# A two-layer gated network on one core: waits, weight loads and transform order at the start and at the batch turns

## The chip, the cores and the metric

One core of one Trainium2 chip runs the whole program. The metric is device time in microseconds, the median over executions; lower is better. A profiled execution has a time of its own.

## The reference, cut to what matters

The input `x` has 4 batches of 512 tokens with 512 features, `ctx` is 4 x 512 x 512. Four sublayers follow each other, each on the layer-normed `x` and each added back with a tanh gate:

```python
x = x + tanh(g_xattn[0]) * moe_by_token_id(layernorm(x), tokens, ctx, ctx, ctx)   # 4 experts: silu(x g^T) * (x u^T), then y d^T
x = x + tanh(g_ffn[0])   * hadamard_ffn(layernorm(x))      # fwht, gate and up 2048 wide, silu, fwht, down
x = x + tanh(g_xattn[1]) * wkv(w, u, layernorm(x), ctx)    # recurrence over the 512 tokens
x = x + tanh(g_ffn[1])   * moe_top2(layernorm(x))          # 8 experts, 448 wide, two per token, and a shared one
```

In `hadamard_ffn` the input is multiplied by signs and passed through a Walsh-Hadamard transform, and so is the hidden layer, before `W_down` (512 x 2048).

## The kernel before, in words

Everything is written out by hand: each engine (TensorE, VectorE, ScalarE, GpSimd, SyncE) has its own list of instructions, and semaphores tie the lists together. An engine does its list in order, so a wait holds everything behind it. Products of float32 are made of three products of rounded high parts and low parts (`wh` and `wl`, `xh` and `xl`).

**First sublayer, called attention here (0 to 160 us).** The tokens are sorted by expert into 19 tiles of 128. VectorE makes a one-hot table from the token ids (`ge`, `mask`, L1479 to L1482), TensorE counts ranks with it (L1084 to L1092), VectorE turns them into row numbers (`from_i`, L1531), and GpSimd gathers the rows of `x` with them (`gather`, L545). The four context matrices come in by DMA; ScalarE rounds each of their 16 blocks (`wh`, L827), VectorE makes the rest (`w_low`, L1523). Block `j` belongs to expert `j // 4`. A tile is then normalized (`x_stats`, `x_norm`, L1555 to L1562), turned on TensorE (`x_turn`, L1102), split (`x_high` on ScalarE, `x_low` on VectorE, L1567), and multiplied (L1116). In the kernel before, TensorE waits for all 16 `wl` blocks and for `s_slot` ahead of the first `x_turn`, and the wait for `mask` (`s_gate`, 2) also counts ScalarE's tanh of the gates (L824), which needs two small loads:

```python
pe.wait_ge(s_gate, 2)
pe.wait_ge(s_wl, E0 * DC)
```

**Between the sublayers (160 to 194 us).** TensorE transforms `W_down` in 16 pieces (`w16`, L1146), whose results ScalarE copies (L925). The pieces are loaded by SyncE in 8 transfers of 512 KB (L434, L467), made of rows of 128 floats, that is of 512 bytes, into four places, so that 4 of them wait for places to come free. Meanwhile the results of the first sublayer are gathered back into token order (L564, four tiles for a batch), added (`residual`, L1605), their deviation is inverted by GpSimd (L534), and `x` is normalized (`xnf`, L1675). TensorE turns it (`turn`, L1157; bank `c` gets chunk `c` of all four tiles), ScalarE scales it (L865), VectorE makes two butterfly steps (`half_mix`, `full_mix`, L1626 to L1633), TensorE the last seven of the transform (`mix`, L1162). Before the mixes stand `w16` 12 to 15, the wait for ScalarE's last copy and two transforms of down weights (`prep_w`, L1151).

**Second sublayer and wkv (194 to 762 us).** Four batches of 16 steps: `gate` and `up` (both `product`, L1178), then `down` of the step before (L1206). Steps of batch 0 also prepare the weights (`gu_high`, `gu_low`, `down_scale`) and keep them in DRAM; the steps of batches 1 to 3 run the wkv of the batch before beside them. The last two steps of a batch also make the four mixes of the next one: in batches 1 and 2 mixes 0 and 1 ahead of `up` of step 14, mixes 2 and 3 ahead of `up` of step 15.

**Last sublayer (762 us to the end)** is the mixture of eight experts. The change does not touch it.

SyncE's list around the change: four loads of `x` (L431), after the first four gathers have landed; after all 16 `wl`, four `W_down` loads (L434); the gate and up weights of chunk 0 (`load_wn`, L439); the 19 stores of results (L446); `load_wn(1, .)`; the other four `W_down` loads; then the keeping of chunk 0 (L458).

## Time and profile before

| what | value |
|---|---|
| median of three executions | 1280.11 us (1280.07 to 1285.75) |
| profiled execution: its own time | 1281.66 us |
| profiled execution: span from first to last instruction | 1279.7 us |
| TensorE matmul busy | 1209.8 us, 95% of the span |
| TensorE weight loads, VectorE, ScalarE, GpSimd busy | 1012.2, 666.1, 450.1, 458.2 us |
| chain of waits, share by engine | TensorE 80%, VectorE 8%, DMA 3%, ScalarE 3%, issue 3%, GpSimd 2% |

The span is cut in 40 slices of 32 us; the busy tenths of TensorE and its granted clock read:

```profile
PE   1999979999999999999999998999889999999998
PEclk9999999999999999999999999998999999999999
```

The first digit is the first 32 us, the sixth holds 160 to 192 us. Matmuls are pipelined and their ends are modelled, so starts of successive groups say more than the length of one.

### The profile page before, as it was taken

The page shows a single profiled execution, that of the slowest core. Times are in us where ns is not written, and L with a number is a line of the kernel's source. Part 1 is how long each engine was busy: PE and PEld are TensorE (multiplying, and loading weights), DVE is VectorE, ACT ScalarE, POOL GpSimd, SP SyncE. Part 2 cuts the span into 40 slices and gives each one's busy share as a digit, 9 for nine tenths or more (in the row PEclk, how much of TensorE's full clock was granted, in tenths as well). Part 3 has the DMA queues.
Part 4 walks back from the last instruction along what each step waited for, and adds up shares of the span by engine and source line. Part 5 has one row for each costly group of instructions (what it writes and reads, how often), then busy time and mean ns, then how long its engine had stood idle before and what let it go on. Part 6 is the DMA issues. An engine that isn't in the chain of part 4 may idle for free.

```text
span 1279.7 us, 17777 instructions
## 1 busy us (share of the span) xinstructions
PE 1209.8 (95%) x5789; PEld 1012.2 (79%) x5790; DVE 666.1 (52%) x1214; ACT 450.1 (35%) x754; POOL 458.2 (36%) x395
## 2 busy tenths in 40 slices
PE   1999979999999999999999998999889999999998
PEld 1788867777788878887788877888778888888887
DVE  6555358745455655576545566867723334333331
ACT  3333343333144432533243526654222222222222
POOL 2221022100013211232043313324776627986665
PEclk9999999999999999999999999998999999999999
DMA  5822176665559974796486613113653624645553
GB/s 194 288 90 68 50 239 255 262 246 198 213 190 336 314 249 159 273 343 248 151 310 235 230 42 107 43 67 145 232 194 133 205 82 164 221 146 173 173 156 132
DMA packets 71657, 241.75 MB, mean 189 GB/s; under 512 B 8428, under 2 KB 18888, under 8 KB 57896
## 3 DMA queue, kind: packets, MB, share of 16 engines
q1 hardware_dynamic: 48312, 155.93, 33.5%
q0 software_dynamic: 22816, 84.72, 20.1%
q8 instruction: 37, 0.61, 0.2%
q10 hardware_dynamic: 464, 0.27, 0.1%
q14 instruction: 28, 0.23, 0.1%
HBM read 165.13 MB, written 75.76 MB: 188 GB/s over the span
## 4 chain that ended last, share of the span: by engine, by line
PE 80%; DVE 8%; issue 3%; ACT 3%; DMA 3%; POOL 2%; ACTq 0%; SPq 0%; POOLq 0%; DVEq 0%
PE bank L1178 25%; PE bank L1342 17%; PE bank L1206 12%; PE bank L1375 9%; PE bank L1116 4%; PE bank L1136 4%; PE bank L1309 2%; PE bank L1360 1%; PE bank L1162 1%; PE bank L1151 1%; POOL xs_sorted L772 1%; DMA xs_sorted<-row,slw 1%; PE bank L1102 1%; PE bank L1157 1%; PE bank L1124 1%
## 5 line engine op out<-in xcount | busy, mean ns | idle before, releaser
L1178 PE MATMUL bank<-xTh,G 128*128 128x512 f32 x1024 | 275.9, 397 | 1.5 <-DVE xTl L1637 1.5
L1178 PEld LDWEIGHTS bank<-xTh,G 128*128 128x128 f32 x1024 | 190.8, 188 | 45.9 <-issue 5.7
L1342 PE MATMUL bank<-W,dxh 128*128 (+2 forms) x880 | 206.0, 377 | 11.3 <-DVE dmid L1799 8.3
L1342 PEld LDWEIGHTS bank<-W,dxh 128*128 128x128 f32 x880 | 163.7, 191 | 26.3 <-issue 11.6
L1206 PE MATMUL bank<-DN,bhh 128*128 128x512 f32 x512 | 158.0, 390 | 0.0
L1178 PE MATMUL bank<-xTl,G 128*128 128x512 f32 x512 | 137.2, 390 | 0.0
L1375 PE MATMUL bank<-W,dhh 128*128 (+1 forms) x440 | 127.1, 411 | 2.3 <-ACT dys L1022 2.1
L1659 DVE SCALAR_TENSOR_TENSOR bs<-bank,tab,bs 128x512 f32<-128x512 f32 x64 | 46.8, 732 | 148.6 <-PE bank L1178 148.6
L1797 DVE TENSOR_TENSOR dmid<-bank,dsg 128x384 f32<-128x384 f32 x55 | 30.6, 556 | 168.6 <-ACT dsg L1012 168.6
L1206 PEld LDWEIGHTS bank<-DN,bhh 128*128 128x128 f32 x512 | 96.2, 188 | 21.5 <-issue 1.9
L1178 PEld LDWEIGHTS bank<-xTl,G 128*128 128x128 f32 x512 | 96.2, 188 | 20.5
L1206 PE MATMUL bank<-DN,bhl 128*128 128x512 f32 x256 | 104.2, 407 | 0.0
L1012 ACT ACTIVATE dsg<-bank 128x448 f32<-128x448 f32 x55 | 29.9, 543 | 210.9 <-PE bank L1342 210.9
L895 ACT ACTIVATE bhh<-bs 128x512 fp32r<-128x512 f32 x64 | 40.3, 630 | 176.5 <-DVE bs L1659 176.5
L1342 PE MATMUL bank<-W,dxl 128*128 (+2 forms) x440 | 100.6, 372 | 0.0
L1375 PEld LDWEIGHTS bank<-W,dhh 128*128 128x128 f32 x440 | 80.4, 193 | 18.9 <-issue 3.4
L889 ACT ACTIVATE bs<-bank,tab 128x512 f32<-128x512 f32 x64 | 44.1, 689 | 143.0 <-PE bank L1178 142.9
L534 POOL TENSOR_TENSOR rstd<-vare,cst 128x4 f32<-128x4 f32 x12 | 12.4, 1032 | 222.3 <-DVE vare L1544 222.3
L1342 PEld LDWEIGHTS bank<-W,dxl 128*128 128x128 f32 x440 | 85.3, 194 | 7.3
L650 POOL TENSOR_TENSOR W<-wst,W 128x1792 fp32r<-128x1792 f32 (+1 forms) x21 | 90.3, 4302 | 0.7
L690 POOL TENSOR_TENSOR cnum<-cnum,cp 128x512 f32<-128x512 f32 x16 | 26.6, 1664 | 139.1 <-DVE cnum L1698 139.1
L1022 ACT ACTIVATE dys<-bank,gates 128x512 f32<-128x512 f32 x55 | 37.9, 689 | 103.5 <-PE bank L1375 103.5
(273 smaller groups left out, 1951.4 us busy)
## 6 DMA issues: line engine op xcount, KB each, us to landing
G<-gate_up_split SPq DMA_DIRECT2D x48, 1024.0 KB, 7.1
DN<-down_split SPq DMA_DIRECT2D x24, 1024.0 KB, 4.9
gate_up_split<-G SPq DMA_DIRECT2D x16, 1024.0 KB, 6.5
wst<-in_L_ffn_w POOLq DMA_DIRECT2D x16, 896.0 KB, 5.7
y_all<-dys SPq DMA_DIRECT2D x55, 256.0 KB, 2.1
xs_sorted<-zero POOLq DMA_DIRECT2D x3, 3328.0 KB, 20.7
xsd<-xs_sorted SPq DMA_DIRECT2D x39, 256.0 KB, 3.2
down_split<-DN SPq DMA_DIRECT2D x8, 1024.0 KB, 4.0
```

The costliest lines, as they stand in the source:

```text
L650: pool.tensor_tensor(w_place(Wl, slot, p, width), w_rows(p, width), f32(w_place(Wh, slot, p, width)), ALU.subtract)\
L889: act.activation(bs[g % 2][:, :], bank[0][:, :], ACT.Silu, scale=tab[:, T_WGT + g % NK:T_WGT + g % NK + 1]).then_inc(s_bs, 1)
L895: act.activation(bhh[g % 2][:, :], bs[g % 2][:, :], ACT.Copy).then_inc(s_bhh, 1)
L1022: act.mul(dys[t % 2][:, :], bank[4][:, :], gates[:, 3:4]).then_inc(s_dy, 1)
L1116: mm = pe.matmul(bank[2 + t % 2][:, :], a[t % 2][:, k, :], w[:, bass.ds(ex * DC + k, 1), :], start=(n == 0), stop=(n == 3 * DC - 1))
L1136: mm = pe.matmul(bank[4 + t % 2][:, :], a[t % 2][:, k, :], w[:, bass.ds(ey * DC + k, 1), :], start=(n == 0), stop=(n == 3 * DC - 1))
L1178: mm = pe.matmul(bank[m][:, :], G[:, c % 2, f, h, m, i, :], a[b % 2][:, i, :], start=(n == 0), stop=(n == 3 * DC - 1))
L1206: mm = pe.matmul(bank[2 + i][:, :], a[g % 2][:, i * P:(i + 1) * P], DN[:, c % 2, f, h, :], start=(k == 0 and n == 0), stop=(k == NK - 1 an ...
L1342: mm = pe.matmul(bank[o][:, 0:width], a[par][:, k, :], w[:, bass.ds(slot, 1), at + k * step:at + k * step + width].rearrange("p a n -> p ( ...
L1375: return pe.matmul(bank[4][:, :], a[par][:, k, :], w[:, bass.ds(slot, 1), W_2 + k * D:W_2 + (k + 1) * D].rearrange("p a n -> p (a n)"), st ...
L1659: dve.scalar_tensor_tensor(out=bs[g % 2][:, :], in0=bank[1][:, :], scalar=tab[:, T_WUP + g % NK:T_WUP + g % NK + 1], in1=bs[g % 2][:, :], ...
L1797: dve.tensor_tensor(dmid[t % 2][:, 0:full], bank[3][:, 0:full], dsg[:, 0:full], ALU.mult)
```

## The change: what it does, and the diff

- **Start.** `mask` has a semaphore of its own, so neither TensorE nor VectorE waits for the tanh, which ScalarE now makes after the 16 roundings; the first `residual` waits for it. TensorE waits for `s_slot` after the first turn, and for the `wl` blocks of a tile's expert ahead of that tile's product. `x_turn(1)` comes after the first product. VectorE makes 8 of the 16 `wl` blocks ahead of the first `x_low` and `x_norm(1)`, and the other 8 behind them.
- **Down weights.** The host lays `W_down` out so that each load has rows of 4 KB. Six of the eight loads stand in the attention (two more places, in `nat`), the last two follow as soon as `w16` 1 and 3 are done, ahead of `load_wn(1, .)`, which now waits until the fourth gather of `y` has landed.
- **First batch.** The 16 transposes of `xnf` go tile by tile, each tile's four behind its own normalization. The mixes stand ahead of the wait for ScalarE's last copy and of `prep_w`. The first gate product of a batch waits for high and low parts chunk by chunk. VectorE makes the low parts ahead of `down_scale`.
- **Batches 1 and 2.** Mix 0 goes behind `up` of step 14, mixes 1 and 2 ahead of `up` of step 15, mix 3 behind it. `normal` goes ahead of `front` on VectorE.

The diff, cut to its core:

```diff
         s_wrow = sem("s_wrow")
-        s_wdn = [sem(f"s_wdn{i}") for i in range(4)]
...
-            nat[:, 1, 2 * n:2 * n + 2, :].rearrange("p a (h c) -> p (a h) c", c=P) for n in range(2)]
-        wd_v = w_down.rearrange("(h a) (c p) -> (a c) h p", a=8, p=P)
+            nat[:, e, 2 * n:2 * n + 2, :].rearrange("p a (h c) -> p (a h) c", c=P) for e in (1, 0) for n in range(2)]
...
             for q in range(4):
                 sp.dma_start(xres[:, 4 * q:4 * q + 4, :], x_v[:, 4 * q:4 * q + 4, :]).then_inc(s_x[q], 16)
             sp.wait_ge(s_wl, E0 * DC)
-            for n in range(4):
-                sp.dma_start(wdn_at[n], wd_v[:, 8 * n:8 * n + 8, :]).then_inc(s_wdn[n], 16)
+            for n in range(6):
+                sp.dma_start(wdn_at[n], w_down[:, 8 * n:8 * n + 8, :]).then_inc(s_wdn[n], 16)
...

+            for n in range(6, 8):
+                sp.wait_ge(s_w16, 2 * (n - 5))
+                sp.dma_start(wdn_at[n - 6], w_down[:, 8 * n:8 * n + 8, :]).then_inc(s_wdn[n - 6], 16)
+
+            sp.wait_ge(s_yg[3], 16)
             load_wn(1, 0)
             load_wn(1, 1)
-            for n in range(4, 8):
-                sp.wait_ge(s_w16, 2 * (n - 3))
-                sp.dma_start(wdn_at[n % 4], wd_v[:, 8 * n:8 * n + 8, :]).then_inc(s_wdn[n % 4], 16)
...
             act.dma_start(gates_raw[:, 2:4], g_ffn.rearrange("(a n) -> a n", a=1).broadcast_to([P, 2])).then_inc(s_gl, 16)
-            act.wait_ge(s_gl, 32)
-            act.activation(gates[:, :], gates_raw[:, :], ACT.Tanh).then_inc(s_gate, 1)
             for j in range(E0 * DC):
                 act.wait_ge(s_ctx[j // DC], 16)
                 act.activation(wh[:, j, :], nat_at[j // DC][:, j % DC, :], ACT.Copy).then_inc(s_wh, 1)

+            act.wait_ge(s_gl, 32)
+            act.activation(gates[:, :], gates_raw[:, :], ACT.Tanh).then_inc(s_gate, 1)
...
                         turn_high(b + 1, step_at(k, 3), 6)
-                    if b + 1 < NB and k >= NK - 2:
-                        for c in range(2):
-                            mixed_high(b + 1, 2 * (k - NK + 2) + c, 6 + c)
+                    if b + 1 < NB and k == NK - 1:
+                        mixed_high(b + 1, 1, 6)
+                        mixed_high(b + 1, 2, 7)
                     if step_at(k, 3) is not None:
                         exps(DC * (b - 1) + step_at(k, 3))
                     hidden_high(g)
+                    if b + 1 < NB and k >= NK - 2:
+                        mixed_high(b + 1, 3 * (k - NK + 2), 6)
                     if k == 1:
...
-            pe.wait_ge(s_gate, 2)
+            pe.wait_ge(s_mask0, 1)
...
             mm.then_inc(s_rank, 1)
-            pe.wait_ge(s_wl, E0 * DC)
-            pe.wait_ge(s_slot, 1)

             def x_turn(t):
                 pe.wait_ge(s_xn, t + 1)
@@ -1103,11 +1105,14 @@
                 mm.then_inc(s_xT, 1)

             x_turn(0)
+            pe.wait_ge(s_slot, 1)
             for t in range(NT0 + 2):
-                if t + 1 < NT0:
+                if 0 < t < NT0 - 1:
                     x_turn(t + 1)
                 if t < NT0:
                     ex = pe.value_load(tex_i[0:1, t:t + 1], min_val=0, max_val=E0 - 1)
+
+                    pe.wait_ge(s_wl, ex * DC + DC)
                     pe.wait_ge(s_xl, t + 1)
                     wait(pe, s_mid, t - 1)
                     n = 0
@@ -1117,6 +1122,8 @@
                                            start=(n == 0), stop=(n == 3 * DC - 1))
                             n += 1
                     mm.then_inc(s_up, 1)
+                if t == 0:
+                    x_turn(1)
                 if 1 <= t <= NT0:
                     pe.wait_ge(s_mid, t)
...
                     for i in range(DC):
+                        if g % NK == 0 and m == 0 and n < 2 * DC:
+
+                            pe.wait_ge(s_hxh if n < DC else s_hxl, DC * b + i + 1)
                         mm = pe.matmul(bank[m][:, :], G[:, c % 2, f, h, m, i, :], a[b % 2][:, i, :],
                                        start=(n == 0), stop=(n == 3 * DC - 1))
                         n += 1
                 return mm

             def gate(g):
-                if g % NK == 0:
-                    pe.wait_ge(s_hxl, DC * (g // NK) + DC)
                 wait(pe, s_bs, g)
                 product(g, 0).then_inc(s_gt, 1)
...
             pe.wait_ge(s_y, NT0)
-            for c in range(DC):
-                turn(0, c, 2 + c)
+
+            for i in range(4):
+                pe.wait_ge(s_xnb, i + 1)
+                for c in range(DC):
+                    mm = pe.transpose(bank[2 + c][:, i * P:(i + 1) * P], xnf[:, i, c * P:(c + 1) * P], ident)
+                    if i == 3:
+                        mm.then_inc(s_bT, 1)
             for n in range(12, 16):
                 w16(n)
+            for c in range(DC):
+                mix(0, c, 2 + c)
             pe.wait_ge(s_w16c, 16)
             for f in range(2):
                 prep_w(0, f, 6 + f)
-            for c in range(DC):
-                mix(0, c, 2 + c)

             for g in range(NG):
                 b, k = divmod(g, NK)
@@ -1262,15 +1274,17 @@
                     for c in range(2, 4):
                         pe.wait_ge(s_hxl, DC + c - 1)
                         mix(1, c, 4 + c)
+                if 0 < b < NB - 1 and k == NK - 1:
+                    pe.wait_ge(s_hxl, DC * (b + 1) + 1)
+                    mix(b + 1, 1, 6)
+                    pe.wait_ge(s_co, n + DC)
+                    mix(b + 1, 2, 7)
+                up(g)
                 if 0 < b < NB - 1 and k == NK - 2:
                     mix(b + 1, 0, 6)
-                    mix(b + 1, 1, 7)
                 if 0 < b < NB - 1 and k == NK - 1:
-                    pe.wait_ge(s_hxl, DC * (b + 1) + 1)
-                    mix(b + 1, 2, 6)
-                    pe.wait_ge(s_co, n + DC)
-                    mix(b + 1, 3, 7)
-                up(g)
+                    pe.wait_ge(s_hxl, DC * (b + 1) + 2)
+                    mix(b + 1, 3, 6)
                 if b == 0 and k == NK - 2:
                     pe.wait_ge(s_wdt, 2 * NJ)
                     mix(1, 0, 6)
@@ -1283,8 +1297,6 @@

                     s = step_at(k, 5)
                     wait(pe, s_co, n + s)
-                    if b + 1 < NB and k == NK - 2:
-                        pe.wait_ge(s_hxl, DC * (b + 1) + 2)
...

-            for j in range(4):
+            for j in range(2):
                 w_low(j)
             dve.wait_ge(s_rank, 2)
             chain(dve.tensor_copy(from_f[:, :], bank[4][:, NT0:2 * NT0]))
@@ -1567,20 +1579,18 @@
                 dve.tensor_tensor(xl[t % 2][:, :, :].rearrange("p k n -> p (k n)"), bank[0][:, :],
                                   f32(xh[t % 2][:, :, :]).rearrange("p k n -> p (k n)"), ALU.subtract).then_inc(s_xl, 1)

-            for j in range(4, 10):
+
+            for j in range(2, 7):
                 w_low(j)
             x_stats(0)
-            w_low(10)
-            w_low(11)
+            w_low(7)
             x_norm(0)
             x_stats(1)
-            w_low(12)
-            w_low(13)
+            x_low(0)
             x_norm(1)
-            w_low(14)
-            w_low(15)
+            for j in range(8, E0 * DC):
+                w_low(j)
             x_stats(2)
-            x_low(0)
...
+                if q == 0:
+                    dve.wait_ge(s_gate, 1)
                 dve.wait_ge(s_x[q], 16)
...
             full_mix(0)
+            for c in range(DC):
+                mixed_low(0, c, 2 + c)
             for f in range(2):
                 down_scale(0, f, 6 + f)
-            for c in range(DC):
-                mixed_low(0, c, 2 + c)
             down_low(0)

...
                     down_scale(j + 1, 0, 7)
-                if b < NB - 1 and k >= NK - (2 if b else 1):
+                if b < NB - 1 and k == NK - 1:
                     for c in range(2):
-                        mixed_low(b + 1, 2 * (k - NK + 2) + c, 6 + c)
+                        mixed_low(b + 1, (1 if b else 2) + c, 6 + c)
                 hidden(g)
                 if more and f == 1:
                     down_scale(j + 1, 1, 6)
@@ -1752,6 +1764,8 @@
                 if b == 0 and k == NK - 2:
                     for c in range(2):
                         mixed_low(1, c, 6 + c)
+                if 0 < b < NB - 1 and k >= NK - 2:
+                    mixed_low(b + 1, 3 * (k - NK + 2), 6)
                 if more and f == 0:
...
                     if step_at(k, 2) is not None:
-                        front(n + step_at(k, 2))
                         if b + 1 < NB:
                             normal(b + 1, step_at(k, 2))
+                        front(n + step_at(k, 2))
                     if step_at(k, 3) is not None:
                         sums(n + step_at(k, 3))
...

-LAYOUTS = {'ctx_2048': turned_context, 'L0_ffn_W_gate': turned_weights, 'L0_ffn_W_up': turned_weights,
+def spread_down(a):
+
+    return a.reshape(D // 8, 8, FC, P).transpose(1, 2, 0, 3).reshape(P, D // 8, P)
+
+
+LAYOUTS = {'L0_ffn_W_down': spread_down, 'ctx_2048': turned_context, 'L0_ffn_W_gate': turned_weights, 'L0_ffn_W_up': turned_weights,
```

VectorE at the first tiles (`wl` are the low parts of the context, `xs` normalized rows, `xl` their low parts, `st`, `mv`, `va` the statistics), before:

```order
L1562 TENSOR_SCALAR xs_70<-xg,mv_117,rs_119 128x512
L1555 BN_STATS st_116<-xg 128x6
L1556 BN_AGGR mv_117<-st_116 128x2
L1557 TENSOR_SCALAR va_118<-mv_117 128x1
L1523 TENSOR_TENSOR wl<-nat_late,wh 128x512 x2
L1562 TENSOR_SCALAR xs_71<-xg,mv_117,rs_119 128x512
L1523 TENSOR_TENSOR wl<-nat_late,wh 128x512 x2
L1555 BN_STATS st_116<-xg 128x6
L1556 BN_AGGR mv_117<-st_116 128x2
L1557 TENSOR_SCALAR va_118<-mv_117 128x1
L1567 TENSOR_TENSOR xl_74<-bank,xh_72 128x512
L1567 TENSOR_TENSOR xl_75<-bank,xh_73 128x512
```

and now:

```order
L1535 TENSOR_TENSOR wl<-nat,wh 128x512
L1574 TENSOR_SCALAR xs_70<-xg,mv_117,rs_119 128x512
L1567 BN_STATS st_116<-xg 128x6
L1568 BN_AGGR mv_117<-st_116 128x2
L1569 TENSOR_SCALAR va_118<-mv_117 128x1
L1579 TENSOR_TENSOR xl_74<-bank,xh_72 128x512
L1574 TENSOR_SCALAR xs_71<-xg,mv_117,rs_119 128x512
L1535 TENSOR_TENSOR wl<-nat_late,wh 128x512 x8
L1567 BN_STATS st_116<-xg 128x6
L1568 BN_AGGR mv_117<-st_116 128x2
L1569 TENSOR_SCALAR va_118<-mv_117 128x1
L1579 TENSOR_TENSOR xl_75<-bank,xh_73 128x512
```

The first `xl` was behind all of `wl`; now it and the second `xs` are ahead of eight of them, and the second `xl` is behind these eight.

TensorE between the sublayers (L1146, now L1153: transforms of `W_down`; L1157, now L1240: transposes of `xnf`; `wd`: `prep_w`; `xq`: mixes; `xTh`: the first gate product), before:

```order
L1146 MATMUL bank<-cst,wdn 128x128 x16
L1146 MATMUL bank<-cst,nat 128x128 x16
L1146 MATMUL bank<-cst,wdn 128x128 x16
L1157 MATMUL bank<-cst,xnf 128x128 x16
L1146 MATMUL bank<-cst,nat 128x128 x16
L1151 MATMUL bank<-wd_122,cst 128x512 x2
L1162 MATMUL bank<-xq_130,cst 128x512 x4
L1178 MATMUL bank<-xTh_126,G 128x512 x4
```

and now:

```order
L1153 MATMUL bank<-cst,wdn 128x128 x16
L1153 MATMUL bank<-cst,nat 128x128 x32
L1240 MATMUL bank<-cst,xnf 128x128 x16
L1153 MATMUL bank<-cst,wdn 128x128 x16
L1168 MATMUL bank<-xq_130,cst 128x512 x4
L1158 MATMUL bank<-wd_122,cst 128x512 x2
L1187 MATMUL bank<-xTh_126,G 128x512 x4
```

The mixes stood behind the two `prep_w`; now they stand ahead of them.

TensorE in step 14 of batch 1 (L1178, now L1187: gate and up; `xq`: mixes; `cev`: wkv results), before:

```order
L1178 MATMUL bank<-xTh_127,G 128x512 x4
L1178 MATMUL bank<-xTl_129,G 128x512 x4
L1178 MATMUL bank<-xTh_127,G 128x512 x4
L1162 MATMUL bank<-xq_130,cst 128x512 x2
L1178 MATMUL bank<-xTh_127,G 128x512 x4
L1178 MATMUL bank<-xTl_129,G 128x512 x4
L1178 MATMUL bank<-xTh_127,G 128x512 x4
L1221 MATMUL bank<-cst,cev 128x128 x4
L1206 MATMUL bank<-DN,bhl_139 128x512
```

and now:

```order
L1187 MATMUL bank<-xTh_127,G 128x512 x4
L1187 MATMUL bank<-xTl_129,G 128x512 x4
L1187 MATMUL bank<-xTh_127,G 128x512 x8
L1187 MATMUL bank<-xTl_129,G 128x512 x4
L1187 MATMUL bank<-xTh_127,G 128x512 x4
L1168 MATMUL bank<-xq_130,cst 128x512
L1228 MATMUL bank<-cst,cev 128x128 x4
L1213 MATMUL bank<-DN,bhl_139 128x512
```

Two mixes stood between gate and up; now one stands behind up.

## Rows read from the trace of the kernel before

**Rows 1.** Waits of TensorE, whole span: total us, times, longest us

```profile
PE bank L1102 <- DVE wl L1523: 12.6, 1, 12.6
...
PE bank L1084 <- ACT gates L824: 5.8, 1, 5.8
...
PE bank L1146 <- DMA wdn<-in_L_ffn_W_down: 5.0, 1, 5.0
...
PE bank L1162 <- DVE xq L1632: 1.8, 2, 0.9
```

**Rows 2.** Timeline, 0 to 46 us: start us, us, engine, line, work [idle before]

```profile
4.64 0.23 DVE L1482 TENSOR_TENSOR mask<-ge 128x64 f32<-128x64 f32 x1
...
9.87 0.29 DVE L1485 TENSOR_TENSOR_SCAN upto<-reset,mask 128x64 f32<-128x64 f32 x1 [5.00 <-ACT gates L824]
...
21.64 1.14 POOL L545 DMA_INDIRECT xg<-in_x,from_i  x1 [17.67 <-DVE from_i L1531]
...
28.42 0.55 DVE L1562 TENSOR_SCALAR xs<-xg,mv,rs 128x512 f32<-128x512 f32 x1 [0.49 <-POOL rs L553]
...
32.75 0.69 DVE L1555 BATCH_NORM_STATS2 st<-xg 128x6 f32<-128x512 f32 x1
...
32.89 1.11 PE L1102 MATMUL bank<-cst,xs 128*128 128x128 f32 x4 [12.61 <-DVE wl L1523]
...
34.66 0.69 DVE L1567 TENSOR_TENSOR xl<-bank,xh 128x512 fp32r<-128x512 f32 x1 [0.82 <-ACT xh L835]
```

**Rows 3.** Chain of waits, 0 to 60 us: start us, us, work

```profile
31.63 1.21 DVE wl L1523 x2
...
36.59 4.97 PE bank L1116 x12
...
42.00 2.76 PE bank L1116 x12
```

**Rows 4.** Chain of waits, 159 to 196 us

```profile
165.10 7.79 DMA yg<-y_sorted,slot
...
178.94 1.99 DVE xnf L1675 x4
...
183.00 3.82 PE bank L1146 x32
...
187.49 1.98 PE bank L1151 x4
189.47 3.45 PE bank L1162 x8
...
194.38 1.67 PE bank L1178 x6
```

**Rows 5.** Gathers of x rows, where they land

```profile
DMA to landing us min/median/max: 3.2/3.6/7.3
```

**Rows 6.** Gathers of y rows, where they land

```profile
DMA to landing us min/median/max: 5.0/7.6/9.4
```

**Rows 7.** Windows: us, PE, PEld, DVE, ACT, POOL busy (count), PEclk, DMA share, GB/s

```profile
40.00:42.00 2.00, 2.00 (x10) 1.59 (x9) 0.00 (x0) 0.40 (x1) 0.00 (x0) 1.00 1.05 409
164.00:182.00 18.00, 11.65 (x87) 11.21 (x87) 8.10 (x17) 6.24 (x11) 8.56 (x9) 0.91 1.04 330
...
788.40:791.90 3.50, 3.50 (x11) 2.92 (x12) 3.18 (x6) 0.25 (x1) 0.77 (x3) 0.51 0.28 75
```

**Rows 8.** Timeline, 160 to 200 us: start us, us, work [idle before]

```profile
169.38 0.60 ACT L925 ACTIVATE wd<-bank 128x512 f32<-128x512 f32 x1 [0.30 <-PE bank L1146]
...
181.06 1.94 PE L1157 MATMUL bank<-cst,xnf 128*128 128x128 f32 x16 [1.36 <-DVE xnf L1675]
...
185.68 1.23 DVE L1632 TENSOR_TENSOR xq<-xd 128x1024 f32<-128x1024 f32 x1
...
198.06 1.14 ACT L878 ACTIVATE G<-wn 128x512 fp32r<-128x512 f32 x2
```

**Rows 9.** Timeline of TensorE, 786 to 790 us

```profile
788.39 1.06 PE L1360 MATMUL bank<-cst,dmid 128*128 128x128 f32 x4 [1.96 <-DVE dhh L1808]
```

15 lines of the change are left out of this document (8 added, 7 removed).

## The prediction, as it was put on record

> **What bounds the kernel now.** I read the waits of TensorE first, then the timeline at the places of the longest ones, then the chain of waits. TensorE is busy 95% of the span, so only time in which it stands idle, or runs at the lower of its two clock levels, can be won; the change removes no matmul. Its longest wait, 12.6 us, ends with the last `wl` piece of the context; another of 5.8 us ends with the tanh of the gates; one of 5.0 us ends with a `W_down` load, and two of 0.9 us, in batches 1 and 2, with the butterfly result `xq` [rows 1]. The first two lie in one stretch, the start: until 36.6 us TensorE has not begun its first real product [rows 3]. The third lies in the stretch between the sublayers. There the chain of waits does not run through the `W_down` load but through the gather of the results (7.79 us for one), the normalization, the turns, the last `w16`, `prep_w` and the mixes, up to the first gate product at 194.38 [rows 4]. What counts there is therefore the gathers and the order behind them. From 194 us on the chain is nearly all TensorE.
>
> **The start.** The `mask` is made at 4.64, but the operation behind it starts at 9.87 [rows 2], because the wait includes the tanh. All that follows on VectorE depends on nothing else, so it comes 5.0 us earlier; two `wl` pieces fewer stand ahead of `from_i`, which is worth about 0.4 us, as TensorE's rank product ends only a little before. The first gather goes from 21.64 to about 16.25 [rows 2]. From the first gather to the first `xs` it is 6.8 us, set by GpSimd's four gathers and its power; I keep that: `xs` at 23.0 instead of 28.42. In the kernel before TensorE did not turn it until 32.89 [rows 2]; now it does at 23.7. Turn, rounding and `xl` took from 32.89 to 34.66 + 0.69 = 35.35, that is 2.5 us [rows 2], so the first product can start at 26.2 instead of 36.59. It takes 4.97 us there, where the second takes 2.76 [rows 3]: after a long idle time it runs near the pace of the lower level, 1.2 GHz. It ends at about 31.2.
>
> The second product is the one that counts, since TensorE is dense behind it. VectorE now has eight `wl` pieces of about 0.6 us (1.21 for two [rows 3]), the statistics of tile 2 (0.69 and two small ones, about 1.1) and `xl` of tile 1 in a row: from 26.8 to 33.5; then `xs` of tile 2, 0.55, and the turn on TensorE, 0.6: the product starts at about 34.9 instead of 42.00 [rows 3]. That is 7.1 us at full clock. But TensorE stands idle for about 2.4 us ahead of it. A wait of 1.96 us was followed by a stretch of 3.5 us at 0.51 of the clock [rows 7, 9], so I count on one here too. A whole product at 1.2 GHz would cost 4.97 - 2.76 = 2.2 us [rows 3]; part of the stretch lies in the idle time: I take 1.3. **Start: 5.8 us**, between 4.9 and 7.1.
>
> The tanh moved behind the roundings falls where ScalarE waits for TensorE; nothing. `residual` waits for it at 168, long done.
>
> **Between the sublayers: the gathers.** The gathers of `y` land after 7.6 us (5.0 to 9.4) [rows 6], those of `x` after 3.6 us, 3.2 at the least [rows 5]; the same size, the same queue. The difference is what shares the DMA engines: in 164 to 182 us they are busy all the time (share 1.04) and move 330 GB/s, while in 40 to 42, with rows of 2 KB, they move 409 GB/s at the same share [rows 7]. The 2 MB of `W_down` in 512-byte rows and the 1 MB of the next gate and up weights are what runs beside the gathers. Of these 1 MB in 4-KB rows stays, about 2.5 us at 409 GB/s, half of it ahead of the first gather; the rest is done long before or follows. With 3.7 us instead of the 7.79 on the chain the second gather lands at 168.8 instead of 172.9, and the fourth, issued 2.5 us after it, at 171.3. The additions of the four tiles take 1.4 us each, so the last ends 4.1 us earlier; with 5.0 us, the least of the `y` gathers, 2.7 us. I take **3.8 us**, as the row of the `x` gathers is the nearer one once the loads are gone.
>
> The Trainium skill (DMA: Bandwidth & Descriptors, Specifications) asks for pieces of 512 bytes or more for line rate; by it the old rows were already wide enough and only the amount moved out of the way counts. The trace disagrees in part: 330 against 409 GB/s at one busy share [rows 7]. By that rule the gathers would gain some 1.2 us less, and the sum would be 11.7.
>
> TensorE's own wait for `W_down` (5.0 us) is worth nothing by itself: `w16` 8 to 11 ran beside the gathers and must only be done by the turns. ScalarE copies at one per 0.95 us, the eighth at 169.38 [rows 8], so the twelfth ends at 173.8; the turns come at about 175.5 now. That is near: it would bind if the gathers won 2 us more.
>
> **Turns tile by tile.** The four normalizations take 1.99 us, the 16 transposes behind them 1.94 [rows 4, 8]. At full clock the transposes now run in their shadow, but every bank still gets its last part from tile 3, and ScalarE's four copies (2.4 us) follow as before: 0.4 us. Against it, TensorE is idle from about 173 to 175.5, as long as ahead of the second product, so the clock probably halves here; before, it had fallen during `w16` 8 to 11, where it cost nothing. Then the transposes are the slower ones, and the last bank is late by about 1 us. I take **-0.6 us**, between +0.4 and -1.9.
>
> **Mixes ahead of `prep_w`.** VectorE has the first half of the butterflies at 185.68 + 1.2 = 186.9 [rows 8], TensorE ends the last `w16` at 186.8 [rows 4]; the first mix came at 189.47. It can now come at 186.9; four mixes take 3.45 and the two `prep_w` 1.98 [rows 4], which hide rounding and low part of the last mix (1.4 us). The gate product starts at 192.3 instead of 194.38, counted at unchanged gathers: **2.1 us**. `down_scale` comes 2 us later than the low parts, but its user, the first `down`, comes only after four products of 2.7 us.
>
> **Batches 1 and 2.** The two waits of 0.9 us go [rows 1]: mix 0 comes after `up`, 2.7 us later, when `xq` is there. What is late next is mix 3, behind `up` of step 15: its rounding and low part end some 3 us after `up`, while the mix itself (3.45 / 4 = 0.86 [rows 4]) and `down`, 12 matmuls like a product's (2.76 [rows 3]), keep TensorE for 3.6 us. **1.8 us.** `normal` ahead of `front`: the turn needs both, so nothing; the exps come 1.1 us later, under slack.
>
> **The new wait in SyncE's list** holds `load_wn(1, .)` and the keeping of chunk 0 until about 171. Their user is ScalarE's copy at 198.06 [rows 8], over 20 us later. Nothing.
>
> Sum: 5.8 + 3.8 - 0.6 + 2.1 + 1.8 = **12.9 us**. Against the profiled execution's 1281.66 that is 1268.8; this execution is 1.55 us above the median of 1280.11, so the median should be **1267.2**. The ends of the parts add up to 8.2 and 16.0. The last sublayer is only shifted, but its waits fall differently against the clock: one half-clock stretch of 3.5 us [rows 7] more or less is 1.7 us; I allow 2 us. That gives 1262 to 1274.
>
> **The rivals.**
> 1. *The gathers stay slow.* Four of them at once share the engines with the last two `W_down` loads, which are now issued right ahead of them. For: they are the same engines. Against: the `x` gathers also come four at a time and land after 3.6 us [rows 5]. Gain 9.5: 1270.6. Chance 0.13.
> 2. *The clock stays up* at both places. For: behind the 1.36 us ahead of the turns the transposes ran at 0.12 us each, against 0.28 in the first turn [rows 2, 8]. Against: 1.96 us did [rows 9]. The Trainium skill (TensorE: Matmul & The Clock Gate, HAM oscillation) says that a wait between groups of matmuls can send the array back to half rate, which the rows bear out. Gain 15.2: 1264.9. Chance 0.15.
> 3. *Loads in the attention starve it.* 3 MB of `W_down` and 4 MB of `x` now come while tiles 4 to 7 are gathered. An `x` gather has taken 7.3 us at most [rows 5], and tile 4 has 15 us, so it must take twice that to count. Each tile's wait would cost a few us; gain 6, 1274. Chance 0.07.
> 4. *Slower: the clock does not come back in the attention.* The first product starts, TensorE stops for 2.4 us, and the array stays at 1.2 GHz for the next tiles. A tile of 6.4 us costs 6.4 more; two tiles eat the gain and three end at 1280.1 - 12.9 + 19.2 = 1286.4. Against: the stretch in the rows ended after 3.5 us under dense work [rows 7]. Chance 0.03.
>
> My forecast, the sum within 8 to 16 us, has 0.62. A measurement of this kernel tells about 0.5%, 6.4 us, from no change. Faster by more than that: forecast and rivals 1 and 2, 0.90; within: rival 3, 0.07; slower: rival 4, 0.03.
>
> **What would show it.** The first product near 26 and the second near 35 us; 3 to 4.5 us from issue to landing for the first `y` gathers; no wait for `W_down`; the first gate product about 11 us earlier than 194.4; no wait for `xq` in batches 1 and 2. A second product near 42, gathers still above 7 us, or a new wait of TensorE in the attention would make it wrong.

## The result, and the profile after

The changed kernel takes 1271.35 us (median of six runs, 1266.59 to 1274.89); the kernel before took 1282.39 us beside it (six runs, 1280.07 to 1286.24). The ratio of the runs is 0.9908, 95% interval 0.9885 to 0.9931. The forecast was 1267.2, with a range of 1262 to 1274; by the two medians the gain is 11.0 us, where 12.9 was forecast. The profiled execution took 1271.40 us, its span 1269.3, against 1281.66 and 1279.7 before.

The program was run again later (experiment 12), so the places of the trace can be read twice. All times are us from the start of the span; a gain is what the lead over before grew by in that stretch.

| place | before | after | after, repeat | gain | gain, repeat | forecast |
|---|---|---|---|---|---|---|
| first `w16` (end of the attention) | 160.01 | 155.17 | 154.58 | 4.84 | 5.43 | 5.8 |
| first `xnf` | 178.94 | 172.14 | 170.66 | 1.96 | 2.85 | 3.8 |
| first silu (`bs`) | 197.47 | 189.37 | 187.45 | 1.30 | 1.74 | 1.5 |
| last silu of batch 3 | 755.15 | 741.99 | 740.09 | 5.06 | 5.04 | 1.8 |
| first `dys` (last sublayer) | 793.19 | 780.05 | 778.61 | -0.02 | -0.48 | 0 |
| last `dys` | 1276.46 | 1266.01 | 1260.38 | -2.69 | +1.50 | 0, +/- 2 |
| sum | | | | 10.45 | 16.08 | 12.9 |

So the total of the forecast was close, but three of its terms were not: the gathers brought less, the batches nearly three times as much, and the last sublayer, which the change does not touch, moved by several us.

The 40 slices again. The first one is now busy for 3 tenths where it was 1:

```profile
PE   3999989999999999999999988898999999999998
...
PEclk9999999999999999999999999998899999999999
```

**The start.** Timeline of TensorE, 20 to 46 us (start us, us, line, work, idle before). It answers to [rows 2, 3]:

```profile
24.13 1.11 PE L1104 MATMUL bank<-cst,xs 128*128 128x128 f32 x4 [8.90 <-DVE xs L1574]
26.85 2.07 PE L1121 MATMUL bank<-wh,xl 128*128 x4 [1.61 <-DVE xl L1579]
...
34.73 0.66 PE L1104 MATMUL bank<-cst,xs 128*128 128x128 f32 x4 [1.87 <-DVE xs L1574]
35.71 2.00 PE L1121 MATMUL bank<-wh,xl 128*128 x4 [0.32 <-issue]
...
40.16 0.60 PE L1131 MATMUL bank<-cst,mid 128*128 128x128 f32 x4
...
41.30 1.17 PE L1121 MATMUL bank<-wh,xl 128*128 x4
```

The first product starts at 26.85 where it started at 36.59, the second at 35.71 instead of 42.00. The wait of 12.6 us for `wl` [rows 1] is gone; one of 8.9 for the first `xs` stands in its place. Four matmuls of the second product take 2.00 us where those of the third take 1.17. The windows over it, over the transposes of `xnf` and over the mixes (us, TensorE busy, granted clock, DMA share, GB/s):

```profile
35.70:39.30 3.60, 3.59 (x9) 0.53 1.05 408
...
172.90:176.20 3.30, 3.30 (x18) 0.57 0.98 370
...
181.17:184.70 3.53, 3.53 (x8) 1.00 0.00 0
```

The granted clock is at its lower level of 1.2 GHz in the second product, behind a wait of 1.87 us, and in the transposes, behind one of 4.6.

**Between the sublayers.** Chain of waits, 150 to 192 us; it answers to [rows 4]:

```profile
160.25 5.84 DMA yg<-y_sorted,slot
...
166.12 0.76 DVE xres L1617
...
172.14 0.62 DVE xnf L1687
...
172.90 3.01 PE bank L1240 x13
...
181.17 3.70 PE bank L1168 x8
...
186.58 5.47 PE bank L1187 x24
```

The second gather still stands in the chain, with 5.84 us instead of 7.79; in the repeat it is 4.96. Landing of all sixteen, against 5.0/7.6/9.4 [rows 6] and 3.9/6.9/9.7 in the repeat:

```profile
DMA to landing us min/median/max: 3.8/6.6/10.0
```

The waits of TensorE that the change aimed at, over the whole span. No wait for `gates`, `wl` or a `W_down` load is left, and those for `xq` are 0.2 us in all instead of 1.8 [rows 1]:

```profile
PE bank L1104 <- DVE xs L1574: 10.8, 2, 8.9
...
PE bank L1240 <- DVE xnf L1687: 4.6, 1, 4.6
...
PE bank L1163 <- DVE xnb L1631: 0.4, 1, 0.4
...
PE bank L1168 <- DVE xq L1644: 0.2, 1, 0.2
```

### The profile page after: what moved, and what is told of

The parts are those of the page before. It is cut to its first block, busy times and chain, and to the rows that moved or that the text cites. A ratio compares the mean times of both kernels' runs of the same rounds, so it can differ in the third digit from the quotient of the medians.

```text
span 1269.3 us, 17800 instructions
## 1 busy us (share of the span) xinstructions
PE 1210.6 (95%) x5789; PEld 1014.5 (80%) x5790; DVE 659.9 (52%) x1214; ACT 448.3 (35%) x754; POOL 458.2 (36%) x395
## 4 chain that ended last, share of the span: by engine, by line
PE 81%; DVE 8%; issue 3%; ACT 3%; DMA 2%; POOL 1%; SPq 0%; ACTq 0%; DVEq 0%; POOLq 0%
PE bank L1187 25%; PE bank L1354 18%; PE bank L1213 12%; PE bank L1387 9%; PE bank L1121 5%; PE bank L1143 4%; PE bank L1321 2%; PE bank L1372 1%; PE bank L1168 1%; PE bank L1158 1%; POOL xs_sorted L774 1%; DMA xs_sorted<-row,slw 1%; PE bank L1104 1%; PE bank L1131 1%; PE bank L1365 1%
## 5 line engine op out<-in xcount | busy, mean ns | idle before, releaser
L1187 PE MATMUL bank<-xTh,G 128*128 128x512 f32 x1024 | 275.0, 396 | 0.0
L1187 PEld LDWEIGHTS bank<-xTh,G 128*128 128x128 f32 x1024 | 190.8, 188 | 43.1 <-issue 5.3
L1187 PE MATMUL bank<-xTl,G 128*128 128x512 f32 x512 | 137.1, 390 | 0.0
L1187 PEld LDWEIGHTS bank<-xTl,G 128*128 128x128 f32 x512 | 96.1, 188 | 20.5
```

Of the source, the lines that this page charges most:

```text
L1187: mm = pe.matmul(bank[m][:, :], G[:, c % 2, f, h, m, i, :], a[b % 2][:, i, :], start=(n == 0), stop=(n == 3 * DC - 1))
```

## The experiments

Each starts from the changed kernel. The times of single executions differ by several us through the last sublayer alone (last experiment), so the verdicts come from the stretches of the trace: start to first `w16`, first `w16` to first `xnf`, first `xnf` to first silu, first silu to last silu of batch 3. The changed kernel's two profiles give 155.17 and 154.58; 16.97 and 16.08; 17.23 and 16.79; 552.62 and 552.64. What is smaller than these differences is no finding. Experiments 1 to 10 are one execution each.

**1. The start undone.**

```diff
+            pe.wait_ge(s_gate, 1)
...
-            x_turn(0)
+            pe.wait_ge(s_wl, E0 * DC)
             pe.wait_ge(s_slot, 1)
+            x_turn(0)
...
-                if 0 < t < NT0 - 1:
+                if t + 1 < NT0:
                     x_turn(t + 1)
```

with the tanh, and the two halves of `w_low`, back in their old places on ScalarE and VectorE.

> The changed kernel with the start as before (tanh first, all wl pieces ahead of the first turn, old order of VectorE and TensorE), the rest changed. In the changed kernel TensorE's first W_down transform begins at 155.17 us, 4.84 earlier than before, and the first gate product's result is copied 8.10 us earlier. Theory: the two parts are independent, so the first W_down transform goes back to 160.0 and the first silu of batch 0 to within 0.3 us of 194.2 (3.3 us earlier than before, from 197.47). Rival: the start only moved a wait that the W_down loads in the attention would make anyway; then this kernel's attention is slower than before, beyond 160.5. Rival: the six wide loads cost attention nothing and save some; below 159.5.

Measured: 1276.39 us. The first `w16` is back at 160.49; the later stretches are the changed kernel's (16.47, 17.18, 552.74). So the start is worth 5.3 to 5.9 us and does not depend on the rest. The term of 5.8 holds.

**2. `W_down` in 512-byte rows,** at the new places in SyncE's list.

```diff
-                sp.dma_start(wdn_at[n], w_down[:, 8 * n:8 * n + 8, :]).then_inc(s_wdn[n], 16)
+                sp.dma_start(wdn_at[n], wd_v[:, 8 * n:8 * n + 8, :]).then_inc(s_wdn[n], 16)
...
```

> The changed kernel with W_down in its old layout, so that all eight loads have 512-byte rows again, at the same places and times. Theory (width counts in part): the loads in the attention are hidden, the last two hold the y gathers up; first y gather lands 1 to 3 us later than its 3.96 us, the chain to the first gate product is 1 to 3 us longer than in the changed kernel. Rival (only the amount beside the gathers counts, as the rule on pieces of 512 bytes says): within 0.5 us of the changed kernel. Rival: the slow loads disturb the attention too (its end later than 155.2 by over 1 us).

Measured: 1276.12 us, the surplus all in the last sublayer. First `w16` at 154.37, then 16.75 to `xnf` and 17.27 to the first silu. From the first `w16` to the first gate product it takes 30.65 us, against 30.85 and 29.52 in the changed kernel's two profiles, and the gathers land after 6.5 us (median of sixteen) against 6.6 and 6.9: no gain from wider rows shows beyond what these two differ. The narrow rows do keep SyncE longer. The six issues in the attention take it from 31.41 to 45.85 us instead of from 31.89 to 34.82, under work that hides it. The Trainium skill (DMA: Bandwidth & Descriptors, Specifications) puts line rate at 512 bytes and more; the time of this run agrees with it.

**3. No hold of the next gate and up weights.**

```diff
-            sp.wait_ge(s_yg[3], 16)
             load_wn(1, 0)
```

> The changed kernel without SyncE's wait for the fourth y gather, so that 1 MB of gate and up weights is loaded as soon as its place is free, at about 161 us, beside the gathers. Theory: the gathers land later, the chain to the first gate product grows by 1 to 2.5 us. Rival: the gathers are held only by the last two W_down loads and by GpSimd's own issue; no change (under 0.4 us).

Measured: 1275.93 us; from the first `w16` to `xnf` 18.87 us, where all other versions here take 15.5 to 17.0 and the kernel before took 18.93. The gathers in this kernel, and the window in which they land (us, TensorE busy, granted clock, DMA share, GB/s):

```profile
DMA to landing us min/median/max: 4.1/8.6/9.7
```

```profile
164.00:172.00 8.00, 3.34 (x29) 0.91 1.02 365
```

and the same window of the changed kernel:

```profile
164.00:172.00 8.00, 4.32 (x37) 1.00 0.72 236
```

Of the whole edit to the down weights, the gain in this stretch hangs on the one line that keeps 1 MB of other weights behind the gathers: without it nothing is left. With it the DMA engines are no longer full. Whether the line alone would bring the gain, with four `W_down` loads beside the gathers as before, was not run.

**4. The transposes by chunk again.**

```diff
-            for i in range(4):
-                pe.wait_ge(s_xnb, i + 1)
-                for c in range(DC):
+            pe.wait_ge(s_xnb, 4)
+            for c in range(DC):
+                for i in range(4):
...
```

> The changed kernel with the 16 transposes of xnf behind all four normalizations, chunk by chunk, as before. In the changed kernel the first scaled copy began 3.79 us after the first xnf, before 2.79. Theory: TensorE runs at 1.2 GHz there after 4.6 us of idle time in either order, so the transposes take 3.3 us and now start 1.5 us later, but bank 0 is whole after a quarter of them; ScalarE is then paced by TensorE: first copy after 3.2 us, the last one 1 us later than in the changed kernel; the first gate product 0.5 to 1.2 us later. Rival: tile by tile is what costs the 1 us, and the old order brings it back: first copy after 2.8 us, the gate product 0.5 to 1 us earlier than in the changed kernel.

Measured: 1266.64 us, with 18.48 us from `xnf` to the first silu instead of 16.8 to 17.2. Timeline of TensorE and the window:

```profile
172.60 3.65 PE L1240 MATMUL bank<-cst,xnf 128*128 128x128 f32 x16 [4.96 <-DVE xnf L1686]
```

```profile
172.60:175.00 2.40, 2.40 (x12) 0.50 1.03 430
```

The clock falls in both orders, because TensorE waits 3.7 to 5 us in both. Tile by tile is worth 1.3 to 1.7 us *given* that. VectorE has the first half of `xq` at 179.6 here, but TensorE makes `w16` 12 to 15 until 180.84 and only then the first mix: what comes late is the four `w16` behind the transposes. The forecast compared transposes at 1.2 GHz in the new order with transposes at 2.4 in the old one, and came to a loss of 0.6.

**5. `front` ahead of `normal` again.**

```diff
+                        front(n + step_at(k, 2))
...
-                        front(n + step_at(k, 2))
```

> The changed kernel with front ahead of normal on VectorE again, mixes as changed. From the first to the last silu of batches 0 to 3 it was 557.68 us before and 552.62 in the changed kernel. Theory: normal beside GpSimd's limit takes 1.86 us for four pieces where it takes 1.11 without; ahead of front it runs beside nothing. So the four pieces go back to about 1.86 us and the silu interval to 555.3 to 555.6 (2.8 longer). Rival: the order does nothing and the mixes bring all 5 us: interval 552.6.

Measured: 1269.20 us; batches 0 to 3 take 555.36 us instead of 552.6, so this order, which I had costed at nothing, is worth 2.7. TensorE's waits for `xnb` account for 1.5 us of it; no row names the rest. Who waits for the transposes of `xnb` in this kernel (the releaser, us and times of TensorE's idle time before them; above it VectorE's `xnb`, duration ns min/median/max):

```profile
L1631 DVE TENSOR_SCALAR xnb<-xres,mv,rstd x48: 331/341/719, 244.6 to 578.0; 128x128 f32<-128x128 f32 x48
...
  DVE xnb L1631: 1.9, 5
```

and in the changed kernel:

```profile
L1631 DVE TENSOR_SCALAR xnb<-xres,mv,rstd x48: 336/341/346, 246.9 to 575.6; 128x128 f32<-128x128 f32 x48
...
  DVE xnb L1631: 0.4, 1
```

**6. The mixes at their old steps,** and behind `prep_w` in the first batch.

```diff
+                if 0 < b < NB - 1 and k == NK - 2:
+                    mix(b + 1, 0, 6)
+                    mix(b + 1, 1, 7)
...
```

> The changed kernel with the half step taken back (mixes 0, 1 ahead of up of step 14, 2, 3 ahead of up of step 15) and, between the sublayers, prep_w ahead of the mixes. Theory: the silu interval grows by the two mix waits, 2 x 1.2 us, to about 555.0; from the first xnf to the first gate product it is 13.9 in the changed kernel and becomes 16.0 to 16.4. Rival: the mixes do not matter where they stand, since TensorE runs as many matmuls: both within 0.5 us of the changed kernel.

Measured: 1275.35 us; batches 0 to 3 take 555.75 us, and TensorE waits again for `xq`:

```profile
PE bank L1166 <- DVE xq L1642: 2.6, 2, 1.3
```

The half step is worth 3.1 us; with experiment 5 that makes 5.8 where 5.06 was gained, so the two overlap. In the first batch it takes 14.31 us from ScalarE's first copy of the transposes to the first silu, against 13.43 to 13.46 in the changed kernel and in every other run that leaves this stretch alone, and 15.74 before: the mixes ahead of `prep_w` bring 0.9. The other 1.4 belongs to what this run leaves in place, among it the waits chunk by chunk, and which part of it was not run. From the first `xnf` to the first gate product I had expected 16.0 to 16.4 us; it is 13.77, as in the changed kernel (13.88 and 13.44).

**7. Unused products** where TensorE waits: 18 ahead of the first turn, 3 behind it, 19 ahead of the turns of `xnf`. Nothing reads them.

```diff
+            pe.wait_ge(s_wh, 2)
+            for n in range(18):
+                pe.matmul(bank[7][:, :], wh[:, 0, 0:P], wh[:, 1, :], start=True, stop=True)
...
```

> The changed kernel with matmuls whose results nobody uses in TensorE's idle times: 18 of 512 columns ahead of the first turn, 3 behind it, 19 ahead of the turns of xnf. Theory: the first products and these turns run at 1.2 GHz because TensorE was idle. With the filling the first product takes 2.8 to 3.5 us instead of 5.2, the second 2.8 instead of 4.5, so the first W_down transform comes 1.5 to 2.5 us earlier relative to the first gather; the 16 transposes follow their normalizations, and the first gate product comes 0.8 to 1.2 us earlier after the first xnf. Rival: the slowness is that of reading fresh weights or of the DMAs beside it, not of the idle time; the products stay at 5 us and the filling only delays them.

Measured: 1268.24 us; first `w16` at 151.62, 3 to 3.5 us earlier. The windows over the second product and over the transposes:

```profile
33.70:36.60 2.90, 2.85 (x12) 1.00 1.04 400
168.97:170.90 1.93, 1.93 (x19) 1.00 0.85 329
```

Both now run at the upper level, 2.86 us from start to end of the second product instead of 4.45, and 1.91 for the transposes instead of 3.33. From `xnf` to the first silu it is 16.36 us, 0.4 to 0.9 less; the 19 products themselves ran over, so that the transposes began 1.3 us behind the first `xnf` instead of 0.8. The first product was the miss: 2.8 to 3.5 us had been expected, and it took 4.39, most of it still at the lower level:

```profile
25.46:29.85 4.39, 4.39 (x13) 0.63 0.84 259
```

**8. The later `wl` blocks spread over four tiles,** two behind each, and turn 1 ahead of product 0.

```diff
-            for j in range(8, E0 * DC):
-                w_low(j)
...
+                if t in (1, 2, 3, 4):
+                    w_low(2 * t + 6)
+                    w_low(2 * t + 7)
...
```

> The changed kernel with the last eight wl pieces spread over tiles 1 to 4 and the second turn ahead of the first product again. Theory: the second product is late because VectorE makes eight wl pieces (4.9 us) and then xl, and because the second turn comes after the first product; now it can follow the first product at once, 27.9 + 5.2 = 33.1 plus one turn of 0.6, at about 33.8 instead of 35.7, and with no idle time before it at full clock: the first W_down transform 3 to 4 us earlier than 155.17. Rival: expert 2's wl pieces then come too late or the W_down loads behind them meet the y stores; TensorE waits in tiles 2 to 10 and the gain is under 1 us.

Measured: 1283.24 us, slower than before (1281.84 beside it). The second product did run from 32.77 to 35.60, but:

```profile
PE bank L1104 <- DVE xs L1572: 14.1, 3, 8.8
PE bank L1121 <- DVE wl L1533: 9.3, 2, 5.0
```

The third and a later product wait for `wl`. The tokens are not spread evenly over the experts, as I had assumed: their ids go up to 99985 and are clipped to 24999, so that most belong to the last one, and tile 2 already needs blocks that I had put off. The idea fell with the data.

**9. Turn 1 ahead of product 0 with `x_low(1)` and `x_norm(2)` early,** the `wl` blocks before tile 2 all the same; `w16` 12 to 15 ahead of the turns of `xnf`.

```diff
+            w_low(8)
+            x_low(1)
+            w_low(9)
+            x_norm(2)
+            for j in range(10, E0 * DC):
+                w_low(j)
...
```

> The rest of the start is paid by TensorE's order and by VectorE's. Here x tile 1 is turned ahead of product 0, its remainder is taken after two low weights instead of eight, and xn of tile 2 right after it; the conversions 12 to 15 of W_down stand ahead of the four turns of xn on ScalarE. Theory: product 1 follows product 0 without a gap, ends near 37 us instead of 40.16, and the first W_down conversion begins at 151.5 to 152 instead of 154.2 to 155.2. The early conversions 12 to 15 take nothing from the turns of xn, which wait for the gathers anyway, and the pair of later ones isn't missed: from xn to the first silu 16 to 17 us as now (17.2). In all 2 to 3 us, so 1264 to 1268 us by the tail as it falls. Rival A: the later low weights (10 to 15) are then late and the third and fourth products wait for them as in the spread-out kernel, at least 3 us, and the conversions begin at 154 or later. Rival B: conversions 12 to 15 wait for the last W_down load behind the gathers and hold ScalarE, so the turns' copies begin over 1 us later than 3.8 us behind xn.

Measured: 1271.1 us. The start did what was expected: the second product from 33.07 to 35.91, first `w16` at 151.74. The stretch from `xnf` to the first silu did not (17.47 us). Timeline of TensorE and windows over the transposes and over the mixes:

```profile
168.55 1.91 PE L1236 MATMUL bank<-cst,xnf 128*128 128x128 f32 x16
175.40 5.31 PE L1164 MATMUL bank<-xq,cst 128*128 128x512 f32 x8 [4.94 <-DVE xq L1642]
```

```profile
168.50:170.50 2.00, 1.96 (x18) 1.00 0.90 219
175.40:180.60 5.20, 5.20 (x9) 0.68 0.14 59
```

The transposes are quick, but the four `w16` no longer fill the wait for `xq`, and the lower clock now falls on the mixes (5.31 us instead of 3.70). Neither of my rivals had this.

**10. The last `W_down` load held back too,** until the second gather of `y` has landed (on top of 9).

```diff
+                if n == 7:
+                    sp.wait_ge(s_yg[1], 16)
```

> As the kernel with the early start, and the last of the eight W_down loads waits for the second gather of y as well. Theory (the load issued beside the second gather is what makes it land 5.84 us behind its issue where the first took 3.96): the stretch from the first W_down conversion to xn shrinks by 1 to 2 us, from 16 to 17 us to 15 to 15.5, and the first silu comes earlier by as much. Rival: VectorE's residual steps and the two later gathers set xn, the load matters nothing: the stretch stays within 0.5 us; or the last load now lands so late that conversions 14 and 15 hold ScalarE's queue ahead of the turns' copies, and the first silu comes 1 us or more later than in the kernel without this wait.

Measured: 1267.08 us; from the first `w16` to `xnf` 16.18 us against 16.01 in 9, so the stretch did not shrink. The gathers of `y` did get faster, though. Timeline of VectorE's additions, each behind its gather, with VectorE's idle time before it in brackets. In 9, the second and third:

```profile
160.82 0.75 DVE L1615 SCALAR_TENSOR_TENSOR xres<-yg,gates,xres 128x512 f32<-128x512 f32 x1 [0.38 <-DMA yg<-y_sorted,slot]
163.11 0.75 DVE L1615 SCALAR_TENSOR_TENSOR xres<-yg,gates,xres 128x512 f32<-128x512 f32 x1 [0.81 <-DMA yg<-y_sorted,slot]
```

and here, the second to fourth:

```profile
160.73 0.73 DVE L1617 SCALAR_TENSOR_TENSOR xres<-yg,gates,xres 128x512 f32<-128x512 f32 x1
162.11 0.73 DVE L1617 SCALAR_TENSOR_TENSOR xres<-yg,gates,xres 128x512 f32<-128x512 f32 x1
164.89 0.75 DVE L1617 SCALAR_TENSOR_TENSOR xres<-yg,gates,xres 128x512 f32<-128x512 f32 x1 [1.32 <-DMA yg<-y_sorted,slot]
```

From issue to landing the second, third and fourth gather take 4.6, 5.6 and 5.4 us in 9, and 3.4, 3.5 and 5.3 here. No other run has the second under 4.4 or the third under 4.7. So the load is what slows the second and the third. Issued at 160.6 instead of 157.3, it lies beside the fourth, which then sets `xnf`. What the hold wins at two gathers it loses at the fourth; a hold until the fourth gather has landed was not run.

**11. What was left, together:** the start of 9, `w16` 12 to 15 behind the turns as in the changed kernel, unused products at the start as in 7 and 14 ahead of the turns.

> What the runs so far left for the start and for the first batch, together: turn 1 ahead of product 0 and the order of VectorE that goes with it (8.5 us of waits for x rows stay), unused products at the start (18 ahead of the turn of x tile 0 and 3 behind it), and 14 more ahead of the turns of xn; the conversions 12 to 15 stand behind the turns again, where they fill TensorE's wait for xq (4.94 us without them). Theory: W_down's first conversion at 150.5 to 151.7 us, from xn to the first silu 16.0 to 16.8 us instead of 17.2 to 17.5, the first silu at 183 to 184.5 us instead of 189.4; batches 0 to 3 as now (552.7). That is 5 to 6.5 us ahead at the end of the attention and the first sublayer; the last sublayer comes out between 481 and 489 us as its half-clock stretches fall, so the median is 3 to 7 us below the changed kernel's, 0.984 to 0.989 of the kernel before. Rival: the tail takes the lead back (its waits for x rows fall otherwise), and the two can't be told apart: under 2 us between the medians.

Measured: 1265.71 us (five runs, 1265.02 to 1267.57), 0.987 of the kernel before, 0.9835 to 0.9906. First `w16` at 150.99, 15.85 us from `xnf` to the first silu, which comes at 182.30, earlier than in any other. The unused products did nothing for the first product here (5.1 us at a granted clock of 0.51); the second follows it at 32.59 and takes 2.84. At the transposes TensorE no longer waits. Timeline:

```profile
167.20 1.94 PE L1246 MATMUL bank<-cst,xnf 128*128 128x128 f32 x16
```

**12. The changed kernel again,** on the same chip as 11.

> The changed kernel itself, beside the last one on the same chip. Both theories: 0.988 to 0.993 of the kernel before. Its profile shows how far the tail (from the first product of the last sublayer to the last) varies between two executions of one program: if the stretches at half clock are set by the program alone, the tail is within 0.5 us of the 486.0 us of the first profile; if they fall by chance, it differs by 2 to 5 us.

Measured: 1268.84 us (six runs, 1265.89 to 1273.29), 0.9895 of the kernel before, 0.9861 to 0.9929. Experiment 11 is 3.1 us below it by the medians, though the runs of the two overlap (from 1265.9 to 1267.6). Of the profiled executions 11 leads by 5.1 us at the last silu of batch 3 and by 0.6 at the last `dys`. Both beat the kernel before, by under 2%. In the profile, the last sublayer takes 481.77 us from first to last `dys`, against 485.96 in the first profile of the same program. The windows up to the 26th `dys` and behind it, first profile:

```profile
780.00:1033.40 253.40, 236.47 (x1205) 0.95 0.38 135
1033.40:1266.00 232.60, 230.79 (x1184) 1.00 0.50 165
```

and this one:

```profile
778.60:1027.80 249.20, 228.32 (x1196) 0.99 0.39 137
1027.80:1260.40 232.60, 230.71 (x1183) 1.00 0.50 165
```

Behind the 26th the two are alike to 0.02 us. Ahead of it one program took 253.4 us at a granted clock of 0.95 and 249.2 at 0.99; the clock records show the lower level for 23.9 us of that part in the first profile and for 6.8 in this one. So the stretches at 1.2 GHz differ between executions of one program, and the time with them, by 4.2 us here; the theory that the program alone sets them fell. In the profiles of all runs above, none of which touches this sublayer, it takes between 481.7 and 491.7 us.

## Why the prediction was right, and where it was not

- **The start: right.** Forecast 5.8, between 4.9 and 7.1; the trace has 4.84, just under that, and 5.43, undoing it 5.3 to 5.9. The first product came at 26.85 (forecast 26.2), the second at 35.71 (34.9). The lower clock was there as forecast, but took more: 4.45 us for a product instead of 2.76, which is 1.7 where I had taken 1.3. Rival 2, a clock that stays up, did not come about at either place.
- **The gathers: mis-sized.** "With 3.7 us instead of the 7.79 on the chain" is the step that failed. The second gather took 5.84 us (4.96 in the repeat) and stayed in the chain. 3.8 was forecast, with 2.7 as the lower bound; 1.96 and 2.85 came. The sum had the last loads out of the way by then ("half of it ahead of the first gather"), but the last `W_down` load is issued at 160.7, between the first gathers, and lands at 166.6. Experiment 10 shows that it is this load: held back, it leaves the second and third gather 3.4 and 3.5 us, about what the row of the `x` gathers had promised, and slows the fourth instead. So rival 1 had the mechanism, slow gathers through the `W_down` loads, with a price too high: it left the gathers 0.4 us of gain.
- **The rows of 4 KB: wrong.** I read 330 against 409 GB/s at one busy share as a sign that wide rows move faster. Experiment 2 has both widths at the same places, and the stretch takes 30.65 us against 30.85 and 29.52. The windows compared two mixtures of traffic, not two widths.
- **The new wait in SyncE's list: right that it costs nothing, blind to what it brings.** I weighed it as a cost only. Experiment 3 shows it to be the part on which the gathers' gain rests (1.9 to 2.8 us).
- **Turns tile by tile and mixes ahead of `prep_w`: the sum right, the parts not.** -0.6 and +2.1 make 1.5; the trace has 1.30 and 1.74. The parts are +1.3 to +1.7 (experiment 4) and 0.9 (experiment 6), with the slow transposes as forecast, 3.33 us. The first of these is measured against the old order at the lower clock and not against the kernel before, so the two do not add up to the trace. From the first `xnf` to VectorE's `xq` it is 7.75 us (172.14 to 179.89; 7.31 in the repeat) instead of 6.74. Experiment 11, with these transposes at the upper level, has 6.35, so the 0.4 us that the new order was to win are there (6.74 to 6.35) and the lower clock takes 1.0 to 1.4. It takes it in the old order too: 7.92 there (170.48 to 178.40), with the four `w16` behind the transposes slow as well.
- **Batches: the largest miss, 5.06 against 1.8.** Two steps failed. The waits for `xq` are 1.8 us in [rows 1], but putting the mixes back costs 3.1 us, 2.6 of them waits for `xq`. And "`normal` ahead of `front`: the turn needs both, so nothing" is wrong by 2.7: it looked at what the turn depends on, and not at what runs beside `normal`.
- **The last sublayer: allowed for, too narrowly.** "one half-clock stretch of 3.5 us [rows 7] more or less is 1.7 us; I allow 2 us": one program differs by 4.2 us between two executions. In the first profile it gave back 2.69 us, in the second it added 1.50. Most of the difference between 1271.4 and 1265.9 of these executions is there.
- **Rivals 3 and 4: fell.** No wait for x rows in the attention beyond the start. The lower clock did not stay: the window from 35.70 to 39.30 reads 0.53, and the third product runs at the upper level, 1.17 us for four matmuls.
- **The range: its ends are not the sum of the parts' ends.** 8.2 and 16.0 are given. The ends that the terms state add up to 9.6 and 15.2, which with the 2 us for the last sublayer is 1262.9 to 1272.5. The measured 1271.35 lies inside both.

The forecast's total came near by luck, because errors met: in the first profile the batches gave 3.3 us more than forecast, the gathers 1.8, the start 1.0 and the last sublayer 2.7 less.

## What to carry to other kernels

Judge a transfer by what runs beside it: keeping one unrelated MB behind the gathers was worth 2 to 3 us, wider rows nothing that shows. When a load is held back, look at where it lands next: moved from beside the second gather it slowed the fourth, and the sum stayed the same. Where an engine's order is changed, look at what the neighbouring engines do at that moment, and not only at who depends on the result. And read a change stretch by stretch against a repeat of the same program: here an untouched sublayer moved by 4 us, more than any part of the change but two.

## What the runs showed that was not expected

**VectorE beside GpSimd.** The timeline at one step of batch 1, before:

```profile
367.10 1.86 DVE L1619 TENSOR_SCALAR xnb<-xres,mv,rstd 128x128 f32<-128x128 f32 x4
...
367.29 1.59 POOL L686 TENSOR_SCALAR ce<-cd,wlim 128x512 f32<-128x512 f32 x1 [11.28 <-DVE cd L1684]
```

and after:

```profile
357.06 1.11 DVE L1631 TENSOR_SCALAR xnb<-xres,mv,rstd 128x128 f32<-128x128 f32 x4
...
360.19 1.57 POOL L688 TENSOR_SCALAR ce<-cd,wlim 128x512 f32<-128x512 f32 x1 [12.27 <-DVE cd L1696]
```

`front` ends with `cd`, which starts GpSimd's minimum at once. If `normal` comes behind it, the two run together, and the four operations take 1.86 us instead of 1.11, a single one up to 0.72 instead of 0.35; GpSimd loses nothing (1.59 and 1.57). Experiment 5, which changes only this order, has the slow ones again. The Trainium skill (SBUF — State Buffer, SBUF: two separate sides) says that GpSimd and some VectorE instructions share a pair of ports, which one instruction holds to its end while the other waits. The rows agree that the two engines get in each other's way, but not in the wait: the loss is 0.75 us beside an instruction of 1.59, not all of it. That ports are the cause is shown by no run here.

**The clock column in the first product.** Its matmuls run at the pace of the lower level (2.07 us for four, as at 35.71), yet the window over it says 1.00:

```profile
27.00:32.30 5.30, 5.30 (x13) 1.00 0.97 355
```

The trace's clock records begin only at 32.40 us, and ahead of them the column prints 1.00. In experiment 11 they begin earlier, and the first product reads:

```profile
27.10:32.20 5.10, 5.10 (x12) 0.51 1.02 384
```

Durations tell what the column does not.
